# A graph transformer on one core: five buffers for gathered rows in place of four, half the descriptor scratch, and sort steps two slots apart

## The reference, cut to what matters

```python
for l in range(L):                                   # L = 2
    xn = _layernorm(x, ln1_g[l], ln1_b[l])
    xp = xn + xn @ Wpos[l] + bpos[l] + deg[:, None] * Wdeg[l][0] + bdeg[l]
    q, k, v = (xp @ W[l] + b[l] for W, b in ...)     # n x 8 x 16 each
    att = clip(einsum('ehd,ehd->eh', q[dst], k[src]) / scale, -50, 50)
    ex = exp(att - segment_max(att, dst)[dst])
    alpha = ex / (segment_sum(ex, dst)[dst] + 1e-16)
    aggr = segment_sum(v[src] * alpha[:, :, None], dst)
    x = x + (aggr @ Wo[l] + bo[l])
    x = x + (gelu(_layernorm(x, ln2_g[l], ln2_b[l]) @ W1[l] + b1[l]) @ W2[l] + b2[l])
```

## Time and profile before

| | before |
|---|---|
| time, median of 3 runs | 3817.89 us (3809.33 to 3823.78) |
| the profiled execution | 3814.57 us, span 3812.6 us |
| mean granted clock of PE | 0.888 |
| PE busy | 3120.4 us (82%) |
| DVE busy | 2896.4 us (76%) |
| POOL busy | 2513.6 us (66%) |
| ACT busy | 1821.4 us (48%) |
| indirect DMAs of POOL | 2448 |
| first products of layer 0, of layer 1 | 311.39 us, 2142.07 us |

### The profile page before, as it was taken

The page is one execution under the profiler, slowest core; times in us unless marked ns, Lnnn a source line. Parts: engine busy times, 40 slices in busy tenths (PEclk is TensorE's granted clock), DMA queues, the critical chain, the costliest instruction groups (busy, mean ns, idle before and its releaser), DMA issues.

```text
span 3812.6 us, 74017 instructions
## 1 busy us (share of the span) xinstructions
PE 3120.4 (82%) x25398; PEld 2506.9 (66%) x25705; DVE 2896.4 (76%) x6187; ACT 1821.4 (48%) x4404; POOL 2513.6 (66%) x2470
## 2 busy tenths in 40 slices
PE   4984688888898888888887688888888888888887
PEld 3753566667676666776776476666666676766665
DVE  8995678777777877878787387778777777777776
ACT  1331245445354544545555345554555555555555
POOL 1007777677676766767676477776677777777772
PEclk6785789899898989989999799889998989999997
DMA  3024455445454544545454355554555555555552
GB/s 85 23 74 141 117 153 167 138 147 169 127 171 132 171 144 140 165 137 165 143 174 139 103 163 171 169 168 145 159 176 159 164 168 165 176 169 170 165 169 77
DMA packets 427248, 558.53 MB, mean 146 GB/s; under 512 B 78472, under 2 KB 345440, under 8 KB 426676
## 3 DMA queue, kind: packets, MB, share of 16 engines
q0 software_dynamic: 117504, 321.02, 28.7%
q1 hardware_dynamic: 301862, 225.47, 19.6%
q10 hardware_dynamic: 7506, 7.20, 0.6%
HBM read 527.98 MB, written 25.44 MB: 145 GB/s over the span
## 4 chain that ended last, share of the span: by engine, by line
PE 44%; DVE 25%; issue 8%; ACT 7%; POOL 6%; DMA 5%; SPq 2%; DVEq 1%; another core or an unknown queue 0%; POOLq 0%; ACTq 0%
PE psum L952 12%; PE psum L1042 6%; POOL kv_ring L1965 5%; PE psum L993 4%; PE psum L1026 4%; DVE att L1683 4%; PE psum L1063 2%; DVE scratch L1674 2%; PE psum L1009 2%; DVE work L1378 2%; DVE kv_ring L1395 2%; DMA q_win<-q_table 2%; PE psum L1123 2%; PE psum L970 2%; DVE scratch L1698 2%
## 5 line engine op out<-in xcount | busy, mean ns | idle before, releaser
L1965 POOL DMA_INDIRECT kv_ring<-kv_table,src_idx x1840 | 1878.1, 1021 | 732.9 <-issue 543.8
L1228 ACT ACTIVATE scratch<-psum 128x512 f32<-128x512 f32 (+1 forms) x1228 | 679.5, 568 | 553.0 <-PE psum L970 201.0
L1965 POOL DMA_INDIRECT arena<-kv_table,src_idx x608 | 617.2, 1015 | 273.5 <-issue 179.8
L952 PE MATMUL psum<-arena 128*128 128x256 f32 x2156 | 673.1, 435 | 73.1 <-ACT scratch L1228 43.9
L1239 ACT COPY arena<-psum 128x512 f32<-128x512 f32 x616 | 327.3, 532 | 580.5 <-PE psum L952 577.9
L993 PE MATMUL psum<-q_win,scratch 64*128 64x128 f32 x4896 | 410.0, 314 | 169.1 <-DVE scratch L1674 80.4
L952 PEld LDWEIGHTS psum<-arena 128*128 128x128 f32 x2156 | 422.9, 216 | 177.1 <-ACT scratch L1228 58.3
L1683 DVE TENSOR_REDUCE att<-scratch 128x64 f32<-128x1024 f32 (+1 forms) x460 | 536.0, 1165 | 0.1
L993 PEld LDWEIGHTS psum<-q_win,scratch 64*128 64x128 f32 x4896 | 346.8, 214 | 263.7 <-issue 166.5
L1009 PE MATMUL psum<-scratch 128*64 128x136 f32 x4896 | 373.2, 297 | 17.4 <-ACT work L1322 6.3
L1674 DVE TENSOR_TENSOR scratch<-psum,kv_ring 128x1024 f32<-128x1024 f32 x230 | 280.3, 1219 | 139.6 <-DMA kv_ring<-kv_table,src_idx 92.4
(11 more groups left out here) (252 smaller groups left out, 4725.0 us busy)
## 6 DMA issues: line engine op xcount, KB each, us to landing
arena<-kv_table SPq DMA_DIRECT2D x154, 896.0 KB
kv_ring<-kv_table,src_idx POOLq DMA_INDIRECT x1840
q_win<-q_table SPq DMA_DIRECT2D x612, 32.0 KB
work<-kv_table SPq DMA_DIRECT2D x98, 128.0 KB
q_win<-q_table SPq DMA_DIRECT2D x154, 64.0 KB
arena<-kv_table,src_idx POOLq DMA_INDIRECT x608
work<-q_table SPq DMA_DIRECT2D x98, 64.0 KB
kv_table<-work SPq DMA_DIRECT2D x49, 128.0 KB, 2.1
```

The lines of the kernel that those rows point to most:

```text
L952: mm = e.matmul(to[:, t % 2 * 2 * D:(t % 2 + 1) * 2 * D], hot_source[:, t * P:(t + 1) * P], source_rows[:, t, :], start=True, stop=True)
L1228: e.activation(to[:, at:at + width], apart[k % FILL_BANKS][:, 0:width], ACT.Relu, bias=1.0, scale=-1.0).then_inc(apart_read, 1)
L1965: e.indirect_dma_start(kv[m % RING_KV][:, t, :], None, kv_table[l], bass.IndirectOffsetOnAxis(ap=src_idx[:, c * T + t:c * T + t + 1], axis ...
```

## The change

The number of buffers becomes five (four in `kv_ring`, 8 KB more in each partition). The room comes from the scratch for POOL's descriptors, 8192 bytes in each partition in place of 16384. And in every sort but sort 0 the steps 5 to 18 stand two slots apart in place of one; the reading of a bank stays one slot behind its matmul.

```diff
-RING_KV = 4
+RING_KV = 5
...
 SORT_STEPS = 3 * SA + 11
+SORT_EVERY = 2
...
             slots.setdefault(u, []).append((s, k))
-            u += 1
             if k in SORT_BANKED:
-                slots.setdefault(u, []).append((s, -k))
-        assert u + 2 <= 2 * at[s * OB] - 8
+                slots.setdefault(u + 1, []).append((s, -k))
+            u += SORT_EVERY if s and 5 <= k < SORT_STEPS - 4 else 1
+        assert u + 2 <= 2 * at[s * OB] - 8, (s, u, 2 * at[s * OB] - 8)
...
-    nc = _bacc.Bacc("TRN2", target_bir_lowering=False, num_devices=1)
+    nc = _bacc.Bacc("TRN2", target_bir_lowering=False, num_devices=1, dynamic_dma_scratch_size=8192)
```

## The result

| | before | changed |
|---|---|---|
| median of 14 runs each | 3810.86 us | 3794.95 us |
| ratio | 1 | 0.9952, 95% interval 0.9931 to 0.9973 |
| profiled execution: time, span | 3814.57, 3812.6 us | 3806.18, 3804.3 us |
| layer 0, first to last products | 1774.1 us | 1742.5 us |
| products of unit 20 to those of unit 200 | 1405.5 us | 1396.6 us |

The change gained 0.5%, some 18 us, where 93 were forecast (89 against this median). The rival in which the stops only move had 3793. The time also stands at the very edge of the stated range (3662 to 3795); that says nothing for the forecast.

The account below looks back on a forecast made before the run. PE and DVE, waiting for each other, were taken to bound layer 0 while sorts run, POOL its tail. Layer 0 -83 (about 10 from the buffer) and layer 1 -10 gave -93: 3722 us, range 3662 to 3795.

Parts of the forecast that it names:

- the stops only move: Rival: spread ranks meet other banks' readers, clock stays at 0.86, only the tail gains: -21, about 3793 us; chance 0.10.
- The fifth buffer, alone: Layer 0's tail: POOL one chunk further ahead, its run of 20 chunks becomes 19; -11 us.
- The sorts' steps: PE's waits before the sorts' ranks and placings, 6.7 us a sort: spacing removes two thirds, 4.5 us a sort.
- the sign that the prediction names for this: Sign of being wrong: PE's idle time before other groups grown by as much as it fell at the sorts' matmuls.
- The clock: 2.5 us a sort: PE in the sorts' stretches: fewer stops raise the granted clock from 0.86, worth 2.5 us a sort.
- Layer 0's end, 2002: Layer 0's last products: unit 200 at 1846.6, the end at 2002, 83 us earlier.
- POOL and PE together: Layer 0 after the change: these two engines would be what is late next; no size of its own.
- Layer 1, -10: Layer 1's sorts: -7 us from sort 11 and -3 from sort 10, together -10.
- SP, hidden: A sort's table, written 4 to 6 slots before its first load instead of some 20: still hidden, no cost.

Follow-up runs that it names:

- e9: Kernel before with five buffers and the scratch at 8192, sorts' steps one slot apart as before: ratio 0.9955 (0.9935 to 0.9974).
- e5: Kernel before with the sorts' steps two slots apart, four buffers and full scratch: ratio 0.9967 (0.9943 to 0.9991).
- e12: Kernel before with the sorts' comparison done twice, 39 us more of DVE's time: ratio 1.0074 (1.0046 to 1.0101).
- e17: Kernel before with the sorts' comparison filling only 16 of 128 places from the second sort on, 26 us less of DVE: ratio 0.9955.
- e18: Sorts' steps two slots apart (four buffers, full scratch) plus the comparison done twice: ratio to the kernel before 1.0108 (1.0065 to 1.0151).
- e10: Kernel before with five buffers, half the scratch and layer 0's sort steps from a searched table avoiding shared banks: ratio 0.9922 (0.9896 to 0.9947).
- e11: Kernel before with four more matmuls ahead of each of the sorts' 48 rank matmuls: ratio 1.0010 (0.9992 to 1.0029).
- e4: The changed kernel once more, on a chip of 5300 us: ratio to the kernel before 1.0003 (0.9971 to 1.0035).

## Why the prediction was wrong

**The fifth buffer, alone: right.** -11 was forecast, at the tail. With the halved scratch it measured -17 (-25 to -10), and the tail shrank by 9 to 11 us; DVE's waits for gathers there went from 17.6 to 4.8 us (e9).

**The sorts' steps, the step that failed.** "What can go is waiting ... I take two thirds of 6.7, 4.5 us a sort." The two thirds were right as a count of the waits before the sorts' matmuls, which fell by 39.5 us in all. Taking them as time was wrong: in e5, of 44 us that went there, 45 came again before the nodes' matmuls and the edges' sums, and the sign that the prediction names for this, idle time before other groups grown by as much, was met. PE waited there for DVE, say so, and DVE was in the middle of its own queue. The spacing removes no work of DVE; it changes which matmul stands behind it. For some 82 us of forecast gain the spacing has 13. I read PE's 83% in a sort's stretch as slack to be had, without asking what DVE would do sooner. DVE was busy for only 76% there, and that was the trap: it has waits for PE's results of its own, so neither looks full. The doses show that the time follows DVE's work, by 0.7 us (e12, e17) to 1.4 us (e18) for each us, the clock's part with it. PE's dose cost 0.1 us for each us, but most of it was paid by the clock, so it does not weigh PE against DVE. That a chain through both engines is why is my reading. ACT is not excluded: it ends a good part of the moved waits (17.4 us before L1108, 10.0 before L1120), and no dose was given to it.

**The clock: 2.5 us a sort, not given back.** This term failed too. The granted clock of the middle is 0.92 before, 0.92 in e5 and 0.93 in the changed kernel. It varies with the period: 0.96 where a period takes 158 us, 0.91 where it takes 166. The rule of the Trainium skill (TensorE: Matmul & The Clock Gate, A second HAM failure mode: psum-queue depth-cycling), that frequent short stops are enough for an oscillating clock, gives no clock back, and the trace agrees so far: 0.92 with the stops at other places. That the short stops are what held it there no run shows.

**Layer 0's end, 2002.** It came at 2069.14, with the first products 15 us later than in the kernel before (326.61 against 311.39; the change does not touch the head, and e5 and e9 have 309 and 316), and those of unit 20 4 us later. Unit 200 came at 1907.6; the moved stops had 1908.6, the forecast 1846.6. "POOL and PE together" were to be late next; but POOL still waited 111 us for messages of DVE, and the time follows DVE's work.

**Layer 1, -10: not seen.** From its first products to the end it took 1671 us before and 1678 after, and 1651 to 1680 in e5 to e10, without order.

**SP, hidden: right.** PE's waits for `sorted_table` from 484 to 1912 did not grow:

```profile
L939 PE MATMUL psum<-arena,places 128*128 128x512 bf16 x124 | 35.0, 364 | 14.6 <-DMA arena<-sorted_table 14.4
```

They were 19.2 us before.

**The rivals.** "The stops only move" had its mechanism, its tail (2064, and unit 20 was 4 us late, against 2069) and its price right, and a chance of 0.10. What spoke for it, a layer 1 that idles as much without sorts, was in hand. In the kernel before, from the products of unit 245 to those of unit 445, with one sort:

```profile
2280.07:3673.68 1393.61, 1175.66 (x9664) 960.31 (x9793) 1057.74 (x2286) 763.23 (x1851) 1033.76 (x1020) 0.92 0.56 167
```

PE idles 1.09 us a unit there, and 1.04 in layer 0's middle. Whoever sees PE idle as much without the supposed cause has a reason to doubt that removing it gains.

## What to carry over

A wait is worth its length only if what ends it would come sooner. Before moving work off a stop, look at what the releasing engine does during it; if it is working through its own queue, the stop will be found again before another instruction. Two engines that wait for each other can both be far from full; add a known dose to each (here 0.8 to 1 us at 48 places) and see which one the time follows, before the schedule is rebuilt around the other. Read PE's busy time and granted clock beside the dose: one on PE can pay for itself by the clock, and then its low price says little.

## What was not expected

**Work that costs PE almost nothing.** 52 us of extra matmuls cost 4 us. PE's wait before them stays (23.6 us before L1071 in e11, 24.4 before L1070 in the earlier trace rows), but its wait before the placings fell from 35.5 to 32.7 us, and the granted clock of the middle rose from 0.92 to 0.94: most of the dose was paid by faster matmuls elsewhere. One of the queries' spreading (L993) took 300 ns in the mean instead of 308, one of the edges' sums (L1009) 292 instead of 301.

**Chips differ by 40%.** The same kernel takes 3810 or 5300 us; each of the two slow chips was met once. On them DVE and POOL are busy for hardly longer (2902 and 2410 us in e4, 2896 and 2514 in the kernel before on the 3800 us), and PE stands again and again. PE in e4, where it waits for nothing that the profile shows:

```profile
1056.86 0.37 PE L992 MATMUL psum<-q_win,scratch 64*128 64x128 f32 x1 [1.03 <-issue]
1058.29 0.37 PE L992 MATMUL psum<-q_win,scratch 64*128 64x128 f32 x1 [1.06 <-issue]
1059.69 0.37 PE L992 MATMUL psum<-q_win,scratch 64*128 64x128 f32 x1 [1.03 <-issue]
```

One matmul in 1.4 us. Before L992 alone such waits are 234 us in that run (242 times, the longest 16.2), and 9 us before the same line in the kernel before on the 3800 us. Of the chain that ended last the page of e4 puts 25% down to "another core or an unknown queue", that of the kernel before 0%. That PE's instructions come late is my reading; the cause is open. A change has to be judged on both kinds: this one gains 0.5% on one and nothing on the other (e4), the spacing alone 0.3% and 0.6%.
